# Preparing the folded weights of a slot-attention kernel: column sums by a product with ones, and another order of the first stage

## What is computed

```python
x_in = _ln(ctx, lnkv_g, lnkv_b)
k = x_in @ wk + bk
v = x_in @ wv + bv
slots = q_mu + jnp.exp(q_logsig) * _ln(x)
for _ in range(3):
    q = _ln(slots, lnq_g, lnq_b) @ wq + bq
    attn = softmax(einsum('bnd,bkd->bnk', k, q) / scale) + EPS
    upd = einsum('bnk,bnd->bkd', attn / sum(attn, 1), v)
    slots = upd @ wu + bu + prev
    slots = gelu(_ln(slots, lnm_g, lnm_b) @ w1 + b1) @ w2 + b2 + slots
    slots = _ln(slots + cond, lnp_g, lnp_b)
```

## Time and profile before

| | us |
|---|---|
| median of 3 runs | 2311.99 (2311.27 to 2313.33) |
| the profiled execution, its time | 2315.96 |
| the profiled execution, its span | 2314.3 |
| TensorE busy | 2275.8 (98%) |
| VectorE / GpSimd / ScalarE busy | 1501.0 / 1000.7 / 975.7 |
| half 1 of the first stage begins on TensorE | 83.68 |
| half 2 begins | 109.09 |

### The profile page before, as it was taken

How to read it: one execution, slowest core, us unless ns; L and a number is a source line. 1 busy time by engine, 2 the same in 40 slices (tenths; PEclk the granted TensorE clock), 3 DMA queues, 4 the chain that set the end, 5 groups by cost and what they waited for, 6 DMA issues and landing times.

```text
span 2314.3 us, 30355 instructions
## 1 busy us (share of the span) xinstructions
PE 2275.8 (98%) x11317; PEld 1868.5 (81%) x11317; DVE 1501.0 (65%) x3056; ACT 975.7 (42%) x1650; POOL 1000.7 (43%) x1351
## 2 busy tenths in 40 slices
PE   8999999999999999999999999999999999999998
PEld 4788888888888888888888888888888887777886
DVE  6778557656476665769657576874766668764542
ACT  2566543343334333333333433333333345666432
POOL 3566235152453515435453452554535156653200
PEclk9999999999999999999999999999999999999999
DMA  5587000000152000013400001350000012204330
GB/s 202 181 315 283 3 1 1 1 1 1 37 208 79 1 23 5 15 50 128 155 6 21 8 10 55 113 170 5 10 19 1 21 55 81 74 29 146 97 113 19
DMA packets 87122, 158.54 MB, mean 69 GB/s; under 512 B 10801, under 2 KB 33337, under 8 KB 83134
## 3 DMA queue, kind: packets, MB, share of 16 engines
q1 hardware_dynamic: 82838, 150.26, 18.9%
q0 software_dynamic: 2688, 6.31, 0.9%
q10 hardware_dynamic: 1450, 0.04, 0.0%
HBM read 106.21 MB, written 50.37 MB: 68 GB/s over the span
## 4 chain that ended last, share of the span: by engine, by line
PE 81%; DVE 12%; POOL 2%; ACT 2%; issue 2%; DMA 0%; ACTq 0%; DVEq 0%; POOLq 0%
PE ps L218 25%; PE ps L220 25%; PE ps L219 25%; PE ps L1493 3%; DVE moments L1981 3%; DVE slots L2354 1%; DVE zTl L2029 1%; DVE tbuf L2341 1%; DVE tbuf L2348 1%; PE ps L444 1%; DVE mx L2303 1%; ACT prob L1885 1%; PE ps L1478 1%; PE ps L431 0%; PE ps L433 0%
## 5 line engine op out<-in xcount | busy, mean ns | idle before, releaser
L218 PE MATMUL ps<-zTh,kTl 128*128 128x512 f32 (+1 forms) x912 | 332.2, 364 | 2.9 <-ACT prob L1885 2.2
L220 PE MATMUL ps<-zTh,kTh 128*128 128x512 f32 (+1 forms) x912 | 324.6, 356 | 0.0
L219 PE MATMUL ps<-zTl,kTh 128*128 128x512 f32 (+1 forms) x912 | 324.3, 356 | 0.0
L218 PE MATMUL ps<-vh,prob_lo 128*128 128x512 f32 x768 | 304.6, 397 | 0.0
L220 PE MATMUL ps<-vh,prob_hi 128*128 128x512 f32 x768 | 299.9, 390 | 0.0
L219 PE MATMUL ps<-vl,prob_hi 128*128 128x512 f32 x768 | 299.2, 390 | 0.0
L2474 POOL TENSOR_SCALAR rs_m<-mv_m 128x1 f32<-128x1 f32 x96 | 60.2, 627 | 526.6 <-DVE mv_m L1983 526.6
L2029 DVE TENSOR_TENSOR zTl<-ps,zTh 128x512 fp32r<-128x512 f32 x224 | 151.0, 682 | 188.4 <-ACT zTh L1750 188.4
L1732 ACT ACTIVATE zbuf<-slots,rs_m 128x512 f32<-128x512 f32 x96 | 78.4, 816 | 333.7 <-POOL rs_m L2479 333.7
L1885 ACT ACTIVATE prob<-ps,nb 128x1024 f32<-128x1024 f32 x96 | 107.3, 1117 | 250.0 <-DVE nb L2308 246.0
L218 PEld LDWEIGHTS ps<-zTh,kTl 128*128 128x128 f32 x912 | 172.1, 189 | 35.1 <-DVE zTl L2029 7.1
(11 more groups left out here) (325 smaller groups left out, 5467.6 us busy)
## 6 DMA issues: line engine op xcount, KB each, us to landing
ctx<-in_ctx_dram SPq DMA_DIRECT2D x8, 1024.0 KB, 7.6
slots<-in_x_dram SPq DMA_DIRECT2D x8, 1024.0 KB, 6.7
kT_d<-kTh SPq DMA_DIRECT2D x6, 1024.0 KB, 8.1
kT_d<-kTl SPq DMA_DIRECT2D x6, 1024.0 KB, 10.6
s_d<-slots SPq DMA_DIRECT2D x6, 1024.0 KB, 5.2
v_d<-vh SPq DMA_DIRECT2D x6, 1024.0 KB, 9.2
v_d<-vl SPq DMA_DIRECT2D x6, 1024.0 KB, 11.2
kTh<-kT_d SPq DMA_DIRECT2D x3, 2048.0 KB, 11.0
```

What stands on the lines that cost most here:

```text
L218: nc.tensor.matmul(out, ll, rh, start=start, stop=False)
L219: nc.tensor.matmul(out, lh, rl, start=False, stop=False)
L220: return nc.tensor.matmul(out, lh, rh, start=False, stop=stop)
```

## The change

- Weights wk and wq are loaded as a quarter, a quarter and a half, to other places in memory. Eight matmuls of ones (`WARM`) stand ahead of all others on TensorE. Folds 0 and 1 now take their quarters in turn.
- Weights times a vector: VectorE (`weighted`, for wu and wk) or GpSimd (for wq and w1) multiplies each of the four chunks by its column and adds them up; TensorE then sums over the partitions by one matmul with a square of ones (`row_sums`, result in all partitions at once) or by four with a column of ones (`col_sums`). The way through DRAM is gone, for all but cond + b2. Four rows are instead loaded to all partitions at the start.
- The key folds' high parts go to ScalarE, and low parts are one step on VectorE. Value folds stand as 4, three units, 5, 6, 7.
- The lists of the first half are in another order on all engines; the column sums of w1 move from half 1 to half 2, their adding up stands on GpSimd behind the first slots of half 0, and `scale_w1` one half later.

The diff, cut to the loads, sums and lists that matter (VectorE's removed lines are mostly left out):

```diff
-            load_weight("wkT", "wst_a", 0); load_weight("wqT", "wst_a", 0)
-            load_weight("wkT", "wst_b", 1); load_weight("wqT", "wst_b", 1)
+            load_weight("wkT", "wst_a", 0, 1); load_weight("wqT", "wst_a", 0, 1)
+            load_weight("wkT", "wst_q", 1, 1); load_weight("wqT", "wst_q", 1, 1)
+            load_weight("wkT", "wst_b", 2, 2); load_weight("wqT", "wst_b", 2, 2)
...
-            sp.dma_start(c0_d, c0out[0:1, 0:1]).then_inc(sem("rows_out"), 16)
-            sp.wait_ge(sem("rows_out"), 3 * 16)
-            sp.dma_start(rows[:, 3, :], rows_d[0].partition_broadcast(P)).then_inc(sem("rows_in"), 16)
-            sp.dma_start(rows[:, 2, :], rows_d[1].partition_broadcast(P)).then_inc(sem("rows_in"), 16)
-            sp.dma_start(rows[:, 0, :], rows_d[2].partition_broadcast(P)).then_inc(sem("rows_in"), 16)
-            sp.dma_start(rows[:, 1, :], a["qmu"].partition_broadcast(P)).then_inc(sem("rows_in"), 16)
-            sp.dma_start(c0[:, :], c0_d[0, :].partition_broadcast(P)).then_inc(sem("rows_in"), 16)
+            sp.wait_ge(sem("wu_shifted"), 4 + C)
+            sp.dma_start(cb_d, conds[:, :]).then_inc(sem("cb_in"), 16)
+
+            sp.wait_ge(sem("pfold"), C)
+            sp.wait_ge(sem("row_step"), UK_ROW + C)
+            sp.wait_ge(sem("acc_step"), ADDS)
             load_weight("w1f", "wst_c")
 
...
+                elif e == 1:
+                    pe.wait_ge(sem("wst_q"), 2 * 16)
+                elif e == 2:
+                    pe.wait_ge(sem("wst_b"), 2 * 16)
+                fold_part(0, e); fold_part(1, e)
+            for u in (2, 3):
                 for e in range(C):
-                    if u == 0 and e == C // 2:
...
-            def col_product(w, col, out):
+            def col_sums(src, out):
                 for t in range(C):
-                    for c in range(C):
-                        last = nc.tensor.matmul(out[:, t:t + 1], wst[w][:, c, cut(t)], col[:, c:c + 1],
-                                                start=(c == 0), stop=(c == C - 1))
-                return last
-
-            def row_product(w, col, bk_):
+                    last = nc.tensor.matmul(out[:, t:t + 1], src[:, cut(t)], ones[:, :], start=True, stop=True)
+                last.then_inc(sem("pcol"), 1)
+
+            def row_sums(src, out):
+                nc.tensor.matmul(out, square[:, :], src, start=True, stop=True).then_inc(sem("pcol"), 1)
...
+                    if u == C:
+                        pe.wait_ge(sem("wu_shifted"), 3 + e)
+                    fold_part(u, e)
+
+            def first_units():
+                pe.wait_ge(sem("fold_step"), C - 1)
+                value_fold(4)
+                pe.wait_ge(sem("fold_step"), C)
+                pe.wait_ge(sem("brow_read"), 2)
+                pe.wait_ge(sem("lo_c"), 4)
+                unit(0, 0); unit(0, 1); unit(0, 2)
+
+                pe.wait_ge(sem("row_step"), VB + C)
+                row_sums(acc[0][:, :], bank(7))
+                value_fold(5)
+                pe.wait_ge(sem("fold_raw"), 1)
+                value_fold(6)
+                pe.wait_ge(sem("fold_raw"), 2)
+                value_fold(7)
+                pe.wait_ge(sem("row_step"), UK_ROW + C)
+                pe.wait_ge(sem("rows_ready"), 1)
+                row_sums(acc[1][:, :], bank(7))
+                row_sums(craw[:, 3, 0:1], bank(6)[:, 0:1])
+                unit(0, 3)
+                pe.wait_ge(sem("acc_step"), ADDS)
+                pe.wait_ge(sem("rows_ready"), 3)
+                col_sums(acc[0], bank(6))
+                pe.wait_ge(sem("fold_step"), 2 * C)
+                unit(0, 4); unit(0, 5)
+                pe.wait_ge(sem("cols_step"), 1)
+                c_transpose(1, 0)
+                c_transpose(1, 1)
+                unit(0, 6)
+                c_transpose(1, 2)
+                c_transpose(1, 3)
+                unit(0, 7)
...
+            act.wait_ge(sem("rows_in"), 4 * 16)
+            A.activation(rows[:, 0, :], rows[:, 0, :], ACT.Exp).then_inc(sem("brow_read"), 1)
+            for u in range(C, 2 * C):
+                value_hi(u)
             act.wait_ge(sem("cols_step"), 2)
             kv_hi(0, 0)
+            c_norm(1, 0)
             kv_hi(0, 1)
-            c_norm(1, 0); c_norm(1, 1)
+            c_norm(1, 1)
             kv_hi(0, 2)
-            c_hi(1, 0); c_norm(1, 2)
-            x_norm(0, 0); c_norm(1, 3)
+            c_norm(1, 2)
+            c_norm(1, 3)
             kv_hi(0, 3)
+            c_hi(1, 0)
+            kv_hi(0, 4)
             c_hi(1, 1)
-            x_norm(0, 1)
-            kv_hi(0, 4)
-            c_hi(1, 2); x_norm(0, 2)
             kv_hi(0, 5)
+            x_norm(0, 0)
+            c_hi(1, 2)
             c_hi(1, 3)
             kv_hi(0, 6)
+            x_norm(0, 1)
+            x_norm(0, 2)
+            kv_hi(0, 7)
             x_norm(0, 3)
...
+            def weighted(n, out, w, col):
+
+                dve.wait_ge(sem("row_step"), n)
+                V.tensor_scalar(out[:, :], wst[w][:, 0, :], col[:, 0:1], None, ALU.mult).then_inc(sem("row_step"), 1)
+                for c in range(1, C):
+                    dve.wait_ge(sem("row_step"), n + c)
+                    V.scalar_tensor_tensor(out[:, :], wst[w][:, c, :], col[:, c:c + 1], out[:, :], ALU.mult, ALU.add)                        .then_inc(sem("row_step"), 1)
+
...
+                c_lo(0, i)
+
+            dve.wait_ge(sem("wst_c"), 2 * 16)
+            row_products(0, "wvT", 0, craw[:, 2, 0:C], "bv", vb)
+            dve.wait_ge(sem("row_step"), C + 1)
+            V.tensor_scalar(vb[:, :], vb[:, :], 1.0 / (D * SHIFT), None, ALU.mult).then_inc(sem("row_step"), 1)
+            dve.wait_ge(sem("wu_shifted"), 2 + C)
+            weighted(VB, acc[0], "wu", vb)
+            row_products(VB + C, "wkT", 0, craw[:, 0, 0:C], "bk", kb)
+            row_products(KB_COL, "wqT", 1, craw[:, 1, 0:C], "bq", uu)
+            dve.wait_ge(sem("wu_shifted"), 3 + C)
+            dve.wait_ge(sem("pcol"), 3)
+            V.scalar_tensor_tensor(rows[:, 2, :], rows[:, 2, :], 1.0 / (D * SHIFT), bank(7), ALU.mult, ALU.add)                .then_inc(sem("rows_ready"), 1)
+            dve.wait_ge(sem("rows_ready"), 1)
+            value_raw(4)
+            dve.wait_ge(sem("row_step"), UU_COL)
+            V.tensor_tensor_reduce(out=junk[:, 0:C], in0=uu[:, :], in1=kb[:, :], scale=1.0, scalar=0.0,
+                                   op0=ALU.mult, op1=ALU.add, accum_out=craw[:, 3, 0:1]).then_inc(sem("row_step"), 1)
+            weighted(UK_ROW, acc[1], "wkT", uu)
+            value_raw(5)
+            value_lo(4)
+            value_raw(6)
+            value_lo(5)
+            c_stats(1, 0)
+            value_raw(7)
+            value_lo(6)
+            value_lo(7)
+            dve.wait_ge(sem("pcol"), 4)
+            V.tensor_tensor(rows[:, 3, :], bank(7), rows[:, 3, :], ALU.mult).then_inc(sem("rows_ready"), 1)
+            dve.wait_ge(sem("pcol"), 5)
+            V.tensor_copy(c0[:, :], bank(6)[:, 0:1]).then_inc(sem("rows_ready"), 1)
+            dve.wait_ge(sem("rows_ready"), 2)
+            dot_m(0, 0)
+            dve.wait_ge(sem("pcol"), 6)
+            V.tensor_copy(r1[:, :], bank(6)[:, 0:4]).then_inc(sem("cols_step"), 1)
             dve.wait_ge(sem("cols_step"), 1)
...
+            c_stats(1, 1); c_stats(1, 2); c_stats(1, 3)
             kv_lo(0, 0)
-            for i in range(2, 4):
-                c_stats(1, i)
-            x_stats(0, 0); x_stats(0, 1)
-            x_stats(0, 2); x_stats(0, 3)
+            dot_m(0, 1)
+            dot_m(0, 2)
             kv_lo(0, 1)
-            dve.wait_ge(sem("rows_in"), 5 * 16)
-            fold(4)
-            dot_m(0, 0); dot_m(0, 1)
-            fold(5)
-            dot_m(0, 2); dot_m(0, 3)
+            dot_m(0, 3)
             kv_lo(0, 2)
-            fold(6)
-            fold(7)
-            c_lo(1, 0); dot_m(1, 0)
+            x_stats(0, 0)
+            c_lo(1, 0)
             kv_lo(0, 3)
-            c_lo(1, 1); dot_m(1, 1)
+            x_stats(0, 1)
+            c_lo(1, 1)
+            kv_lo(0, 4)
+            x_stats(0, 2)
+            kv_lo(0, 5)
+            x_stats(0, 3)
+            c_lo(1, 2)
+            c_lo(1, 3)
+            dot_m(1, 0); dot_m(1, 1)
+            kv_lo(0, 6)
+            dot_m(1, 2); dot_m(1, 3)
             c_stats(2, 0)
-            kv_lo(0, 4)
-            dot_m(1, 2)
-            c_lo(1, 2)
             c_stats(2, 1)
-            dot_m(1, 3)
...
+            def weighted(n, out, w, col):
+
+                G.tensor_scalar(out[:, :], wst[w][:, 0, :], col[:, 0:1], None, ALU.mult).then_inc(sem("acc_step"), 1)
+                for c in range(1, C):
+                    pool.wait_ge(sem("acc_step"), n + 2 * c - 1)
+                    G.tensor_scalar(part[:, :], wst[w][:, c, :], col[:, c:c + 1], None, ALU.mult)                        .then_inc(sem("acc_step"), 1)
+                    pool.wait_ge(sem("acc_step"), n + 2 * c)
```

(7 more changed lines are left out.)

306 lines of the change are left out of this document (139 added, 167 removed).

## The result

The changed kernel takes 2323.78 us in the median of five runs (2320.79 to 2325.24), the kernel before, beside it on the same chip, 2311.53 (2311.27 to 2313.33). The ratio is 1.0045, with a 95% interval of 1.0033 to 1.0056: 0.45% slower, 10.4 us by the ratio (the two medians themselves lie 12.25 us apart). The forecast was 2320.1, slower by 8.1.

What follows compares the result with a forecast made beforehand. TensorE, busy 98% of the span, was taken as the bound; 14.96 us of its work removed less 3.8 added is more than spent on waits, so +8.1 on the median of 2311.99 gives 2320.1 us, range 2309 to 2325.

Steps and rivals of the forecast that it cites:

- mark against before: Forecast: half 2's start on TensorE 8.1 us later; measured: SP's issue of the gp_row load after the first stage.
- To half 0's first units: Start to value fold 4: GpSimd's four wu shifts of 1.93 us set the pace, fold 4 ending at 30.5.
- VectorE's pace in the folds: Half 0's value folds: VectorE ready for fold 7 at 46.1 against 46.4, up to 1 us perhaps lost.
- The four dots: VectorE in half 1, ahead of half 2's statistics: four dot_m at 1.43 us, slowed beside GpSimd's first_slots.
- rival 1: Little sharing of the port between VectorE and GpSimd: +2.7, 2314.7, no measurable change; chance 0.27.
- The adding-up: GpSimd's accw of w1 behind the last first_slots: 11.9 us, ending at 104.0, with rstd_x(1) queued behind it.
- VectorE's list to the last `c_lo`: VectorE's work ahead of half 2: 8.1 us from 108.2, to 116.3.
- rival 2: The clock: TensorE's wait before half 2 brings half rate, up to 1.7 us more; +9.8, 2321.8; chance 0.13.
- Both of the dips that I had foreseen: Clock drops after TensorE's waits before half 1's unit 1 (covered by the later wait) and before half 2.
- Rival 3: Faster: GpSimd's scale steps are in time, half 2 starts at 102.1, 7.0 us ahead; 2305.0; chance 0.10.
- The idle time: Sign: TensorE's idle time in the first 120 us rises by about 19 us (11.1 saved + 8.1 lost).

Runs made afterwards that it cites:

- e6: Changed kernel plus ten matmuls whose result nobody reads in TensorE's 2.38 us wait ahead of half 2; ratio 1.0032 to the kernel before.
- e5: Changed kernel, w1's adding-up before rstd_x(0), half 2's statistics and rstd_c(2) before dots and first_slots, half 3's context load issued earlier; 2310.52 us, ratio 0.9988 to before.
- e10: Kernel before with only w1's product moved to GpSimd's adding-up behind first_slots(0,3) and column sums ahead of half 2; ratio 1.0013 to the kernel before.
- e1: Changed kernel with GpSimd's adding-up of w1 moved ahead of rstd_x(0), into its idle stretch; ratio 1.0030 to the kernel before.
- e2: Changed kernel with VectorE's four statistics of half 2 ahead of c_lo(1,2), c_lo(1,3) and the dots; ratio 1.0034 to the kernel before.
- e3: Changed kernel with half 2's statistics ahead of c_lo(1,2), c_lo(1,3) and the dots, and rstd_c(2) ahead of first_slots; ratio 1.0058 to the kernel before.
- e7: Changed kernel without the eight warming matmuls (WARM = 0); one run, 2325.39 us.
- e12: Changed kernel with the three queue moves (w1's adding-up, half 2's statistics, half 3's context load), measured again unchanged; 2310.69 us, ratio 0.9988 to the kernel before.

## Why the prediction came out as it did

The direction and the chain were right, the size was short by 2.4 us at the mark. Step by step:

| step of the forecast | forecast | measured |
|---|---|---|
| value fold 4 done, units begin | 30.5 | 28.41 |
| `col_sums` of half 0 done | 54.7 | 56.3 |
| `rstd_c(1)` ends | 59.6 | 61.76 |
| half 1 begins | 77.5 | 79.50 |
| four `dot_m` | 4 x 1.43 = 5.7 | 1.56 + 1.55 + 1.14 + 1.52 = 5.8 |
| statistics of half 2 end | 87.1 | 89.17 |
| unit 1 of half 1 | 90.3 | 92.85 |
| last `first_slots` | 92.1 | 93.8 |
| adding-up of w1 | 11.9, to 104.0 | 11.5, to 105.2 |
| `rstd_x(1)` ends | 106.1 | 107.2 |
| half 2 begins | 117.2 | 117.88 |
| mark against before | +8.1 | +10.5 |

- **To half 0's first units** the shifts were over-sized: 6.21 us for the four in place of 4 x 1.93 = 7.7. The lead of 2.1 us was gone by the end of the folds.
- **VectorE's pace in the folds** was the step most in error: "up to 1 us may be lost here", and TensorE waited 1.73 + 1.06 us for `foldf`. From fold 4's end to the end of `col_sums` it is 27.9 us in place of 24.2. VectorE's two late steps:

```profile
42.40 0.75 DVE L2071 SCALAR_TENSOR_TENSOR foldf<-ps,columns,rows 128x512 f32<-128x512 f32 x1
43.81 3.44 DVE L2060 SCALAR_TENSOR_TENSOR acc<-st_wkT,columns,acc 128x512 f32<-128x512 f32 x3
```

The first wait ended with the step at 42.40. What stands ahead of that step had been slow: one 128x4 product of 1.28 us (0.16 at its other two places), and three row products of 1.05 in place of 0.69. The second wait followed wk's `weighted`: I had costed both at 0.75 an operation, and wu's three took 2.33 us, but wk's three 3.44. All of these slow operations lie beside GpSimd's work, most beside its adding-up of wq (38.21 to 50.05). I read it as the sharing that I had charged to the dots alone; no run separates it. By it all steps to half 1 are 1.6 to 2.2 us late.
- **The four dots** were right to 0.1 us, so rival 1 (little sharing) fell: it needed 0.77 each.
- **The adding-up** was 0.4 us cheaper than summed. From the last `first_slots` on, the chain is the forecast's own, and its lateness shrinks from 1.7 to 0.7 us; VectorE's list to the last `c_lo` gave the rest of that (7.5 us in place of 8.1). That half 2's start comes within 0.7 us of the forecast is thus in part luck: 2.1 us won on the shifts, 3.7 lost in the folds and 1.0 won at the end nearly cancel.
- **The clock** is the other part. I gave rival 2 a chance of 0.13 and a price of 1.7 us, and left it out of the sum. It came, at this price: first unit of half 2 4.42 us long (117.88 to 122.30) in place of 2.72. e6 shows that the wait is part of its cause: filled with matmuls, it left the clock at 1.00. Half 2's start at +8.8 and 1.7 are the 10.5. Both of the dips that I had foreseen were there, the one at 93 covered as I said. What I had cited of the Trainium skill ("TensorE: Matmul & The Clock Gate", on oscillation), that idle gaps bring the array back to half rate, the trace and e6 bear out for this gap; e5, whose last gap of 1.88 us left the clock at 1.00, shows that not every gap does it.
- **Rival 3** (the lead is kept) was the other side. e5 goes part of the way to it, by moves that the change does not have: -2.2 us at the mark, where the rival had -7.0. So the loss was the price of where the work stands, not of work.
- **The idle time** in the first 120 us rose by 14.4 us (95.2 us busy against 109.6), where I had asked for about 19. The warming adds 3.8 us of busy time that does no work; counted as idle it makes 18.2.

The median lies 3.7 us above the forecast, within the range. 2.4 of it is the mark's; the other 1.3 is no more than the runs of one kernel differ by.

## What to carry to other kernels

Work taken from the busiest engine is worth nothing until the start of the next stage is followed through every in-order queue: here 11 us less for TensorE became 10.5 us more. A reduction of 11.5 us on GpSimd in front of a 2 us step that others wait for did part of it (alone in the kernel before it costs 3.6 us, e10), the statistics behind the dots and the load behind the store the rest, and with all three moved the loss became a gain of 2.2. Fill an engine's idle stretch that is already there, ahead of its next wait, and look on the DMA queue too: a load behind a store inherits all that the store waits for. Waits in a row don't add, so moves that look poor without the others (2.7 for e1, 1.9 for e2, -1.1 for e3, which has e2's in it) gave 12.7 once the last wait in the row was moved too.

## What the runs showed of the hardware

**The port, operation by operation.** In the changed kernel VectorE's dots have two inputs in SBUF, as GpSimd's slot operations have. VectorE, and then GpSimd:

```profile
79.36 1.56 DVE L2098 CUSTOM_DVE_ANT_0 tbuf<-zc,rows 128x512 f32<-128x512 f32 x1
81.07 1.55 DVE L2098 CUSTOM_DVE_ANT_0 tbuf<-zc,rows 128x512 f32<-128x512 f32 x1
82.55 0.68 DVE L2106 TENSOR_TENSOR vl<-ps,vh 128x512 fp32r<-128x512 f32 x1
```
```profile
79.08 1.29 POOL L2569 TENSOR_TENSOR slots<-slots,rows 128x512 f32<-128x512 f32 x1
80.32 1.75 POOL L2567 TENSOR_TENSOR slots<-slots,rows 128x512 f32<-128x512 f32 x1
```

The dot issued at 79.36 ends at 80.92, 0.55 us behind the end of GpSimd's operation (80.37): it waited and then ran. GpSimd's next, begun at 80.32, takes 1.75 where one alone takes 1.29, and ends 1.15 behind the dot. The second dot ends at 82.62, 0.55 behind that (82.07). `vl<-ps,vh`, with one input in PSUM, takes its 0.68 beside the same work. The Trainium skill ("SBUF — State Buffer", on who contends) says that the shared ports are held for a whole instruction while the other engine waits; a dot alone takes 0.69 and a slot operation 1.29, so the rows agree with it within some 0.15 us. I had left open that the stretch could by this rule be longer than my sum. It was not: in these rows GpSimd's operations wait as well, and the two engines take turns.

**The clock.** A wait of 2.38 us (changed kernel), or of 1.17 (e7), ahead of the eight one-column sums was followed by a granted clock of 0.50, the lower of the two levels, in half 2's first unit (119 to 121 us in both). In e5, with 1.88 us and a stage without longer stops before it, it was not: from 100 to 120 us the mean granted clock is 1.00. So the last wait alone does not decide it. Nor does the kernel alone: half 1's first unit and the step to its transposes took 2.95 us in e5 (79.82 to 82.77) and 4.24 in e12 (79.88 to 84.12), which is the same kernel in another execution. There a later wait hid the difference, and the marks agree to 0.04 us. The 1.65 us that e1, e2, e6 and e7 show is steadier: 3.68 us from the sum row on in e1 and e6, which had no idle time ahead of the sums, 5.34 in e2 and e7, which had 1.04 and 1.17. What decides it is left open.
